# The last unit and the two last top networks get a hand-written end

## The reference, cut to what matters

```
e    = stack(tbl_f[ids[:, f]] for f in range(26))          # 2048 x 26 x 64, gathered
x    = layer_norm(dense @ Wd.T)                            # 2048 x 128
y    = layer_norm(e @ Ws.T)                                # per table row, 64 -> 128
y    = layer_norm(einsum("bne,pn->bep", y, Wsi))           # 26 features -> 32, per sample
T    = concat([x[:, None, :], swapaxes(y, 1, 2)])          # 33 vectors of 128
Z    = T @ T.T, lower triangle                             # 528 products per sample
z    = layer_norm(Zflat @ Wl.T), first 384 of 512
h    = relu(concat([z, dense]) @ W_top1 + b1)              # 640 -> 512 (with the zero columns dropped)
h    = relu(h @ W_top2 + b2)                               # 512 -> 256
out  = h @ W_top3                                          # one number per sample
```

## Time and profile before

| | us |
|---|---|
| median of 3 runs | 583.63 (581.57 to 585.77) |
| the profiled execution | 580.7 |
| its span, first to last instruction | 578.9 |
| PE busy | 512.3 (88%) |
| DVE busy | 441.1 (76%) |
| POOL busy | 400.1 (69%) |
| ACT busy | 270.7 (47%) |
| mean granted clock of PE | 0.968 |

### The profile page before, as it was taken

One profiled execution on the slowest core, in us unless ns is written; L12 is line 12 of the kernel. 1 busy time (PEld: TensorE's weight loads), 2 busy tenths in 40 slices (PEclk: granted clock), 3 DMA queues, 4 the chain that ended last, 5 costly groups with the idle time before them and its releaser, 6 DMA issues.

```text
span 578.9 us, 18338 instructions
## 1 busy us (share of the span) xinstructions
PE 512.3 (88%) x7229; PEld 430.0 (74%) x7229; DVE 441.1 (76%) x861; ACT 270.7 (47%) x647; POOL 400.1 (69%) x420
## 2 busy tenths in 40 slices
PE   2489789999998989989899989989898989999786
PEld 1475568888886868778697868878686868878575
DVE  5388888888887878878688877878787887878611
ACT  1125354645554554636345544636445454646322
POOL 6777777777777777777777777777777777774000
PEclk9778989999999999999899998999999999999889
DMA  3536333434353343434344342434344343433210
GB/s 92 154 120 126 62 65 65 77 65 73 61 77 57 55 81 55 69 62 65 54 75 63 56 78 50 64 64 74 55 75 64 55 75 55 65 64 59 49 21 1
DMA packets 89993, 39.02 MB, mean 67 GB/s; under 512 B 76146, under 2 KB 79858, under 8 KB 89970
## 3 DMA queue, kind: packets, MB, share of 16 engines
q1 hardware_dynamic: 76658, 25.06, 20.0%
q0 software_dynamic: 13312, 13.66, 18.4%
HBM read 29.76 MB, written 8.92 MB: 67 GB/s over the span
## 4 chain that ended last, share of the span: by engine, by line
POOL 56%; issue 20%; DVE 11%; PE 8%; ACT 3%; DMA 2%; DVEq 0%; ACTq 0%
POOL rows L436 56%; DVE y_sum L1012 2%; PE p_y L447 2%; DMA rows<-in_table,index 2%; DVE feat L1025 1%; DVE ut_low L979 1%; DVE var_e L987 1%; PE p_u L522 1%; DVE prod L984 1%; ACT y_sq L781 1%; PE p_b L464 1%; PE p_z L594 1%; PE p_b L469 1%; PE p_b L466 1%; DVE wk_low L952 1%
## 5 line engine op out<-in xcount | busy, mean ns | idle before, releaser
L436 POOL DMA_INDIRECT rows<-in_table,index x416 | 399.9, 961 | 129.2 <-issue 126.0
L522 PE MATMUL p_u<-wsi_c,rows_n 128*128 128x192 f32 (+4 forms) x512 | 86.5, 315 | 0.7 <-DVE rows_n L994 0.6
L1025 DVE TENSOR_TENSOR feat<-p_y,y_rs 128x1024 f32<-128x1024 f32 x64 | 78.4, 1225 | 7.2
L1012 DVE TENSOR_REDUCE y_sum<-y_sq 128x32 f32<-128x1024 f32 x64 | 77.9, 1217 | 6.2 <-ACT y_sq L781 1.9
L522 PEld LDWEIGHTS p_u<-wsi_c,rows_n 128*128 128x128 f32 x512 | 80.8, 200 | 1.3 <-DVE rows_n L994 1.2
L781 ACT ACTIVATE y_sq<-p_y 128x1024 f32<-128x1024 f32 x64 | 64.8, 1012 | 2.9 <-PE p_y L562 2.9
L719 ACT COPY et<-p_t 128x512 f32<-128x512 f32 (+1 forms) x64 | 32.1, 501 | 72.1 <-PE p_t L498 71.7
L533 PE MATMUL p_q<-gram,et 128*128 128x128 f32 x416 | 62.8, 293 | 2.9 <-ACT et L719 2.8
L533 PEld LDWEIGHTS p_q<-gram,et 128*128 128x128 f32 x416 | 56.0, 205 | 4.2 <-ACT et L719 4.2
L498 PE MATMUL p_t<-eye,rows 128*128 128x128 f32 x208 | 35.5, 285 | 26.0 <-DMA rows<-in_table,index 25.9
L594 PEld LDWEIGHTS p_z<-feat 128*32 128x32 f32 x4096 | 46.4, 110 | 16.3 <-issue 12.2
(11 more groups left out here) (137 smaller groups left out, 811.1 us busy)
## 6 DMA issues: line engine op xcount, KB each, us to landing
products<-zs SPq DMA_DIRECT2D x64, 136.0 KB
zb<-products SPq DMA_DIRECT2D x64, 136.0 KB
rows<-in_table,index POOLq DMA_INDIRECT x416
dense_x<-in_dense SPq DMA_DIRECT2D x16, 128.0 KB
wl<-in_Wl_rows SPq DMA_DIRECT2D x1, 1280.0 KB, 6.7
w<-in_W SPq DMA_DIRECT2D x2, 512.0 KB
masks<-in_masks SPq DMA_DIRECT2D x1, 960.0 KB, 6.8
w1z<-in_W SPq DMA_DIRECT2D x1, 768.0 KB, 4.5
```

The costliest lines, as they stand in the source:

```text
L436: pool.indirect_dma_start(out=rows[:, j, g, :], out_offset=None, in_=a["table"], in_offset=bass.IndirectOffsetOnAxis(ap=index[:, n, t, g % ...
L522: last = nc.tensor.matmul(p_u[:, NP * (lo - UH * of):NP * (hi + 1 - UH * of)], rows_n[:, t, :, :].rearrange("r h d -> r (h d)"), wsi_c[:, ...
L1012: nc.vector.tensor_reduce(y_sum[:], y_sq[:], AX, ALU.add).then_inc(y_summed, 1)
L1025: nc.vector.tensor_tensor(feat[:, (j - 1) % UB, :, 2:SLOTS], p_y[:].rearrange("e (b p) -> e b p", p=NP), y_rs[:].unsqueeze(2).to_broadcast ...
```

## The change: what it does

All four queues leave their common body behind unit 62: the loop now runs to n = 14, pass 15 runs with j = 0 to 2, and everything from the gather of unit 63 on is a function `ending()` of each engine (POOL's queue is not touched). Against the order above:

- **PE**: u(62) is cut in two, with q(63) between its first two parts and the rest; the transposes of batch 14's products stand ahead of the high part of y(62), except the fifth chunk, which stands behind u(63) and the bias matmuls of y(63). y(63) goes to `p_t` and `p_q` instead of `p_y`. z(61) comes before u(63). Then: z(62), the dense part of hidden_1 of batch 14 (chunks 3 and 4), z(63), L of batch 14, its `z_hat` and the rest of hidden_1, hidden_2 chunk by chunk, the dense part of hidden_1 of batch 15, the result of batch 14, and batch 15's chain.
- **ACT**: the first copy to `zc` stands ahead of ut_high(62); ut_high(63) ahead of y_sd(62); the squares of unit 63 are two halves. `relu_1` and `relu_2` of batch 14 are DVE's. Of `zc` of batch 15 ACT copies columns 0 to 255 and 512 to 639, DVE 256 to 511 (`zc_shared`). In batch 15's top network three of four `relu_1` and one of two `relu_2` are ACT's, the others DVE's (`h1_shared`, `h2_shared`).
- **DVE**: the variance of unit 63 ahead of ut_low(62); then rows_n(63); then `lower_turned(15)`, which is L1000, L1003 and L1006 of batch 14 (they wait for the fifth chunk, `pack_done`, and for `zt_ready`); then ut_low(63), y_sum(62), y_rs(62), the two halves of y_sum(63), feat(62), y_rs(63), the two halves of feat(63), `normalize_layer` of batch 14, its four `relu_1` and two `relu_2`, its part of `zc`, `lower_turned(16)`, and its share of batch 15.
- **SP**: both last stores, z(62) and z(63), before the two last reads.

The core of the diff (indentation shortened; the first pieces are the shared code, then SP, PE, ACT and DVE; helpers named here carry the same instructions as the lines they replace):

```diff
+LAST_H1 = (p_y[:, 0:128], p_y[:, 128:256], p_y[:, 512:640], p_t[:, 0:128])
+LAST_H2 = (p_q[:, 0:128], p_z[:, 0:128])
...
-    body(0, 0)
-    body(1, 1)
-    with eng.Fori(2, NB - 1 if peel else NB) as i:
-        body(i, 2)
-    if peel:
-        body(NB - 1, NB - 1)
-    body(NB, NB)
-    body(NB + 1, NB + 1)
+def iterations(eng, body, ending):
+    body(0, 0, range(UB))
+    body(1, 1, range(UB))
+    with eng.Fori(2, NB - 1) as i:
+        body(i, 2, range(UB))
+    body(NB - 1, NB - 1, range(UB - 1))
+    ending()
...
+        of = NB - 1
+        store(of, 1)
+        sp.wait_ge(zc_ready, 2 * of)
+        sp.sem_inc(read_begun, 1)
+        for m in range(2):
+            sp.wait_ge(z_stored[m], 32 * of + 16)
+            read_quarter(of, m)
+        store(of, 2)
+        store(of, 3)
+        for m in range(2):
+            sp.wait_ge(z_stored[m], 32 * of + 32)
+            read_quarter(of, 2 + m)
...
-                layer_matmuls(NB - 1, NB - 1)
-            if j == 1 and n == NB:
-                turn_z_hat(NB)
-                pe.wait_ge(dt_ready, 2 * NB)
-                pe.wait_ge(hz_ready, NB - 1)
-                for m in range(4):
-                    last = hidden_1(NB, m, (0, 1, 2, 3, 4), p_y[:, 128 * m:128 * m + 128])
...
+        pe.wait_ge(gathered[3], 32 * PAIRS[3] * NB)
+        pe.wait_ge(et_ready, k)
+        for m in range(PAIRS[3]):
+            last = nc.tensor.transpose(
+                p_t[:, 128 * m:128 * m + 128],
+                rows[:, 3, 2 * m:2 * m + 2, :].rearrange("r g d -> r (g d)"), eye[:])
+        last.then_inc(et_put, 1)
+        pe.wait_ge(rows_ready, k)
+        pe.wait_ge(ut_low_ready, k - 1)
+        partial_sums(2, parts_of_u(2)[:2], True)
+        pe.wait_ge(et_ready, k + 1)
+        pe.wait_ge(q_used, k)
+        for m in range(PAIRS[3]):
+            last = nc.tensor.matmul(p_q[:, 128 * m:128 * m + 128], et[:, m, :], gram[:], start=True, stop=True)
+        last.then_inc(q_done, 1)
+        partial_sums(2, parts_of_u(2)[2:], False).then_inc(u_done, 1)
+        pe.wait_ge(y_ready, k - 1)
+        bias_of_y(in_p_y)
+        pe.wait_ge(zc_ready, 2 * i - 1)
+        pe.wait_ge(xt_ready, NB)
+        for c in range(KC - 1):
+            last = turn_products(c, p_a[:, 128 * c:128 * c + 128])
+        last.then_inc(zt_done, 1)
+        pe.wait_ge(ut_high_ready, k)
...
+        products(k - 2, k - 1)
+        pe.wait_ge(h2_ready, 2 * (i - 1))
+        result(p_b[0:1, 256:384])
+        pe.wait_ge(rows_ready, k + 1)
+        partial_sums(3, parts_of_u(3), True).then_inc(u_done, 1)
+        pe.wait_ge(q_used, k + 1)
+        bias_of_y(in_p_t_p_q)
+        pe.wait_ge(zc_ready, 2 * i)
+        pe.wait_ge(out_ready, i - 1)
+        turn_products(KC - 1, p_b[:, PACK:PACK + 128]).then_inc(pack_done, 1)
+        pe.wait_ge(ut_high_ready, k + 1)
+        high_of_y(in_p_t_p_q)
+        pe.wait_ge(ut_low_ready, k + 1)
+        low_of_y(in_p_t_p_q)
+        products(k - 1, k)
+        hidden_1_half(NB, 0, (3, 4), True, False)
+        hidden_1_half(NB, 1, (3, 4), True, False)
+        products(k, k + 2)
+        layer_matmuls(i, i)
+        turn_z_hat(NB)
+        pe.wait_ge(hz_ready, NB - 1)
+        for half in range(2):
+            hidden_1_half(NB, half, (0, 1, 2), False, True).then_inc(h1_half_done, 1)
+        for c in range(4):
...
+        for m in range(4):
+            hidden_1(NB + 1, m, (3, 4), LAST_H1[m], start=m != 1, stop=False)
+        pe.wait_ge(h2_ready, 2 * (NB - 1))
+        result(p_u[0:1, 256:384])
+        for c in range(KC - 1):
+            if c == 0:
+                pe.wait_ge(zc_ready, 2 * i + 1)
+            if c == 2:
+                pe.wait_ge(zc_shared, 1)
+            last = turn_products(c, p_a[:, 128 * c:128 * c + 128])
+        last.then_inc(zt_done, 1)
+        pe.wait_ge(zc_ready, 2 * i + 3)
+        turn_products(KC - 1, p_b[:, PACK:PACK + 128]).then_inc(pack_done, 1)
+        layer_matmuls(NB, NB)
...
+        act.wait_ge(u_done, k)
+        act.wait_ge(y_done, k - 1)
+        nc.scalar.copy(ut_high[:], p_u[:]).then_inc(ut_high_ready, 1)
+        act.wait_ge(var_ready, k + 1)
...
+        act.wait_ge(y_done, k)
+        act.wait_ge(y_summed, k - 1)
+        nc.scalar.activation(y_sq[:].rearrange("e b p -> e (b p)"), p_y[:], ACT.Square).then_inc(sq_ready, 1)
+        act.wait_ge(out_done, i - 1)
+        put_out(i, p_b)
+        act.wait_ge(z_done, k - 1)
+        act.wait_ge(z_stored[1], 16 * 2 * i)
+        nc.scalar.copy(zs[:, 1].rearrange("r g c -> r (g c)"), p_z[:, 0:GU * SLOTS]).then_inc(zs_ready, 1)
+        act.wait_ge(u_done, k + 1)
+        nc.scalar.copy(ut_high[:], p_u[:]).then_inc(ut_high_ready, 1)
+        act.wait_ge(y_summed, k)
+        nc.scalar.activation(y_sd[:], y_sum[:], ACT.Sqrt, bias=eps_col[:], scale=1.0 / NP).then_inc(y_sd_ready, 1)
+        act.wait_ge(y_done, k + 1)
+        for h, at in ((0, p_t), (1, p_q)):
+            nc.scalar.activation(y_sq[:, UH * h:UH * h + UH].rearrange("e b p -> e (b p)"), at[:], ACT.Square
+                                 ).then_inc(sq_ready, 1)
+        act.wait_ge(y_summed, k + 2)
+        nc.scalar.activation(y_sd[:], y_sum[:], ACT.Sqrt, bias=eps_col[:], scale=1.0 / NP).then_inc(y_sd_ready, 1)
+        act.wait_ge(z_done, k)
+        act.wait_ge(z_stored[0], 16 * (2 * NB - 1))
...
+        lower_turned(i)
+        dve.wait_ge(ut_high_ready, k + 1)
+        nc.vector.tensor_tensor(ut_low[:], p_u[:], ut_high[:].bitcast(F32), ALU.subtract).then_inc(ut_low_ready, 1)
+        dve.wait_ge(sq_ready, k)
+        nc.vector.tensor_reduce(y_sum[:], y_sq[:], AX, ALU.add).then_inc(y_summed, 1)
+        dve.wait_ge(y_sd_ready, k)
+        nc.vector.reciprocal(y_rs[:], y_sd[:]).then_inc(y_rs_ready, 1)
+        for h in range(2):
+            dve.wait_ge(sq_ready, k + 1 + h)
...
+        dve.wait_ge(y_rs_ready, k)
+        dve.wait_ge(z_done, k - UB)
```

More of the change, by code:

```diff
@@ L486, in _, with body @@
             pe.wait_ge(units_ready, 1)
-            def body(i, n):
+            def body(i, n, js):
                 units, layer, top = stages(n)
-                for j in range(UB):
+                for j in js:
                     k = UB * i + j
@@ L646, in body @@
[L646 to L661, removed]
-                        layer_matmuls(i, n)
[L664 to L693, removed]
+                    if j == 3 and layer:
+                        layer_matmuls(i, n)
+            def partial_sums(of, parts, first):
+                for at, (t, lo, hi) in enumerate(parts):
+                    w = SPAN * t - samples_of(t)[0]
+                    last = nc.tensor.matmul(
+                        p_u[:, NP * (lo - UH * of):NP * (hi + 1 - UH * of)],
+                        rows_n[:, t, :, :].rearrange("r h d -> r (h d)"),
+                        wsi_c[:, w + lo:w + hi + 1, :].rearrange("r s p -> r (s p)"),
+                        start=first and at == 0, stop=parts[at] == parts_of_u(of)[-1], skip_group_check=True)
+                return last
@@ new lines, in bias_of_y, with high_of_y @@
+            def bias_of_y(half_at):
+                for h in range(2):
+                    nc.tensor.matmul(half_at[h], bias_w[D * h:D * h + D, :],
+                                     bias_c[D * h:D * h + D].rearrange("r s c -> r (s c)"),
+                                     start=True, stop=False)
+            def high_of_y(half_at):
+                for w in (wy_low, wy_high):
+                    for h in range(2):
+                        nc.tensor.matmul(half_at[h], w[D * h:D * h + D, :],
+                                         ut_high[D * h:D * h + D, :], start=False, stop=False)
@@ new lines, in low_of_y, with products @@
+            def low_of_y(half_at):
+                for h in range(2):
+                    last = nc.tensor.matmul(half_at[h], wy_high[D * h:D * h + D, :],
+                                            ut_low[D * h:D * h + D, :], start=False, stop=True)
+                last.then_inc(y_done, 1)
+            def products(unit, last_of_y):
+                pe.wait_ge(y_ready, last_of_y)
+                pe.wait_ge(zs_ready, unit)
+                for g in range(GU):
+                    for s in range(SQ):
+                        f = feat[:, unit % UB, GU * s + g, :]
+                        last = nc.tensor.matmul(p_z[32 * s:32 * s + 32, SLOTS * g:SLOTS * g + SLOTS],
+                                                f[:, 2:SLOTS], f, start=True, stop=True)
+                last.then_inc(z_done, 1)
@@ new lines, in turn_products, with hidden_1_half, hidden_2 @@
+            def turn_products(c, out):
+                return nc.tensor.transpose(out, zc[:, 128 * c:128 * c + 128], eye[:])
+            def hidden_1_half(n, half, chunks, start, stop):
+                for m in (2 * half, 2 * half + 1):
+                    last = hidden_1(n, m, chunks, p_y[:, 512 * half + 128 * (m % 2):512 * half + 128 * (m % 2) + 128],
+                                    start=start and m % 2 == 0, stop=stop and m % 2 == 1)
```

(7 more changed lines are left out.)

241 lines of the change are left out of this document (187 added, 54 removed).

## The result

The changed kernel takes 591.64 us (589.99 to 592.58, 4 runs) against 583.31 of before: ratio 1.0149, 95% interval 1.0112 to 1.0185. A second set on another chip gave 589.65 (6 runs) and 1.0109 (1.0075 to 1.0143). So it is slower by 1.1 to 1.5%, 6 to 8 us. The sum of the forecast gave +4.3 us, its median was 587.5 and its range went up to 591.0. The sign was right, the size was half to two thirds of what came, and the first median lies above the range.

A forecast was written before the change was run, and what follows sets the result against it. The prediction took the chain behind the last gather, 45.7 us, as what the change can move. Terms 4.5 - 2.1 - 0.9 = +1.5 us plus 2.8 for the clock gave +4.3, forecast 587.5 us, range 583.3 to 591.0.

The forecast's parts named there:

- What bounds the kernel: Behind POOL's last gather: the change can move only the 45.7 us from unit 63's transposes to the last copy.
- The sum at full clock, +1.5 us: Whole tail without clock effects: +4.5 to L(14), -2.1 from there to L(15), -0.9 to the end.
- To rows_n(63), DVE's wait, feat(62), PE's gap: Ahead of z(62): rows_n(63) gains nothing, DVE stands 536.5 to 539.4, feat(62) ends 545.6, PE idles 4.0 us.
- The step that I hold for decisive: DVE's `lower_turned(15)` waits for the fifth chunk, 536.5 to 539.4, with y_sum(62) queued behind it.
- I take two stretches: PE at half clock on z(62), dense part and z(63), then on 24 hidden_1 instructions: +1.4 us each, 2.8 together.
- all gaps here are longer than the two that cost: Argument against the clock staying up: PE's new gaps exceed the earlier 2.9 us and 1.6 and 0.7 us.
- The strict reading of the rule: Throttled is the default and activity releases it; with all three PE gaps punished, a third stretch comes too.
- From L(14) to L(15), -2.1: Batch 14's top network up to L(15) takes 12.3 us instead of 14.5.
- Straight code, nothing: ACT and DVE leave their loops one pass sooner: zero taken, 1 us allowed without the cover of POOL's pace.
- the one that is slower by over 1%: Third half-clock stretch on hidden_1 of batch 15 behind L(15): +5.8 us, 589.4 to 590; chance 0.25, half over 1%.
- the first rival: PE's clock stays up more, one half-clock stretch or none: +1.5 to +2.9 us, 585.1 to 586.5; chance 0.23.
- the third, not slower: Wait at `lower_turned` shorter, L(14) ends within 2 us of before: -1.0 us, 582.6; chance 0.10.

The follow-up runs named there:

- all gaps filled: The changed kernel plus matmuls nobody reads where PE idles: 15 behind y(63), 9 behind L(14), 9 behind L(15); 583.77 us.
- the first gap filled: The changed kernel plus 15 matmuls nobody reads, only behind y(63) on PE; 587.03 us.
- y_sum(62) first: The changed kernel with y_sum(62) ahead of the lowering steps of batch 14 on DVE; 589.64 us.
- the peeled kernel of before: The kernel before, with ACT and DVE leaving their loops one pass sooner, so pass 15 is straight code on all queues; 582.70 us.
- L(14) early: The changed kernel with L of batch 14 moved right behind y(63) on PE, ahead of z(62) and z(63); 581.73 us.
- the one of before with its gaps filled: The kernel before plus matmuls nobody reads in PE's two idle stretches: 12 behind u(63), 6 behind z(63); 580.26 us.

## Why the prediction was right or wrong

- **What bounds the kernel** (right): what the change moved is in the tail. The last gather moved too, but also between kernels that are the same up to it. The reading of the earlier trace rows was not exact: DVE stands 0.39 us ahead of y_rs(62), for ACT's root.
- **The sum at full clock, +1.5 us** (right): the changed kernel with all gaps filled has a tail of 47.1 us against 45.7, +1.4, and its runs are 0.3% above before. Its terms came to +4.7 (forecast 4.5), -2.1 (-2.1) and, from the end of L(15), -1.2 (-0.9).
- **To rows_n(63), DVE's wait, feat(62), PE's gap** (right in time): 3.0 us of wait, 3.9 us of gap, feat(62) at 14.3 us behind unit 63's transposes (549.7 less 535.4; forecast 545.6 less 531.4, 14.2).
- **"The step that I hold for decisive"** (right in its time, wrong in its weight): the wait on DVE is on the chain, since 1.2 us of work put into it bring z(62) 1.0 to 1.1 us sooner; no run takes out all of it. It is there only because L(14) stands behind z(62) on PE. With L(14) in the gap the same wait of 3.0 us costs nothing against before, so L(14)'s place decides, worth 4.7 us at full clock.
- **The clock, "I take two stretches", 1.4 us each** (wrong, and this is the term that was mis-sized): there were three in both profiles, and they cost 2.0, 2.9 and 1.6 us, 6.5 in sum instead of 2.8. I took each stretch's price from the earlier trace rows, where PE had work without a gap as soon as the clock was down, and the stretches lasted 3.4 us. Here the first began while PE was still idle (0.50 from 547.5, z(62) at 549.75), lasted 6.8 us and still held all through the dense part; the second, 6.8 us too, covered the transposes and all 24 instructions, although PE had a gap of only 0.6 us in it. My own condition, "all gaps here are longer than the two that cost", spoke for three stretches, and I gave the third only as a rival: 1.6 us that the sum has at nothing. With +1.4 at full clock this is the whole tail, 7.9 us against the 4.3 of the forecast.
- **The strict reading of the rule**: I took every one of the three gaps as punished. The changed kernel agrees in both profiles, with three low stretches. It is no rule for one gap, though: two of the same length went unpunished, behind L(14) with the first gap filled and behind L(15) with y_sum(62) first. The Trainium skill, "TensorE: Matmul & The Clock Gate", Part 1, says that the throttled state is the default and activity releases it; that each such gap is punished was my reading of it.
- **From L(14) to L(15), -2.1** (right): in the kernel with all gaps filled the first fill follows L(14) at 554.09 and L(15) begins at 566.53, 12.4 us against the forecast 12.3. The round trip of z(63) took longer than the forecast gave it: in that kernel its data came 0.25 us after ACT was ready to copy them, instead of 0.6 us before. PE needed them only later, so this cost nothing.
- **Straight code, nothing** (right), by the peeled kernel of before.
- **The rivals**: what came is the one that is slower by over 1%, given 0.25 and half of that over 1%. By its text +5.8 us; its mechanism, the third stretch, is there and cost 1.6 us, near its 1.5, but its first two were undersized in the same way. What the first rival (one stretch or none) would have given is what the filled kernel shows; the third, not slower, needs L(14) early, which this order doesn't do. The chances for "within 1%" add up to 0.87, and less 0.03 that is 0.84, not 0.82.

## What to carry to other kernels

When matmuls are moved off a gap of the matrix engine, count twice: the gap's own time on the chain, and the half clock for what follows. Count that second price from the moment at which the clock falls, and look whether the work behind it still has gaps: here a low stretch with a gap in it lasted twice as long as one without, so the price of one earlier example did not carry over. Work whose inputs are ready belongs into the gap. Where none is ready, matmuls that nobody reads are a test of what the clock costs, and here even a gain of 0.5%.

## What the runs showed of the hardware

- The tails of these twelve profiles have sixteen stretches at 0.50. In nine of them PE still stood idle after the clock had fallen (for 0.57 us or more), and these lasted 6.8 us; in the other seven PE was busy without a gap, and these lasted 3.4 us.
- The same gap (2.3 and 0.57 us around a burst of 0.55) was followed by a lower clock in some profiles and not in others: behind L(15) not with y_sum(62) first, but in the changed kernel, twice. So the tail of one execution can miss the mean of the runs by the price of a stretch.
- The last gather of 416 began anywhere from 528.6 to 532.5 us in twelve profiles, with POOL's code the same. Single gathers of 1.1 to 1.4 us stand among those of 0.94, and all 416 took 400.3 us in the kernel before, 402.6 in the changed one and 403.1 in the one of before with its gaps filled. Why some are longer, no run shows.
